# A mixture-of-experts layer on one core: TensorE leaves out the upper half of the second layer where an expert's last tile holds at most 128 rows

## The chip, the cores and the metric

One core of a Trainium2 chip. The metric is the device time of one execution in microseconds. Times inside an execution are counted from the start of its span. TensorE is called PE here, VectorE DVE, ScalarE ACT, GpSimd POOL and SyncE SP; PEld is the weight load of TensorE.

## The reference

The input is (4, 1024, 256) in float32. It is normalised, goes through a small attention block (whose result is added to it), is normalised again, and then goes through eight experts, of which each row uses the two with the largest gate values:

```python
logits = flat @ gate_w + gate_b
topv, topi = lax.top_k(logits, TOP_K)                # TOP_K = 2 of E = 8
topw = softmax(topv)
routing = zeros_like(logits).at[arange(T)[:, None], topi].set(topw)
def body(acc, params):
    W1e, b1e, W2e, b2e, we = params                  # W1e 256 x 1024, W2e 1024 x 256
    h = gelu(flat @ W1e + b1e)
    out = h @ W2e + b2e
    return acc + out * we[:, None], None
final, _ = lax.scan(body, init, (w1, b1, w2, b2, routing.T))
x = x + _layernorm(final)
```

With the inputs of this case the experts 0 to 7 are chosen by 585, 110, 3998, 173, 2449, 188, 554 and 135 rows, 8192 in all.

## The kernel before

The first part (up to about 200 us) computes attention and gate and sends each row, by an indirect DMA, to a place in `sorted_x` that belongs to its expert. `steer_table` then works out on DVE, for each expert, how many tiles of TM = 256 rows it has and which number its first tile has. The result, tiles + 32 * base, is the word that each engine reads from `steer`.

The second part is the loop over experts and tiles. `over_tiles` writes it for each engine: it loads the word of expert e, calls `first` for the first tile and `tile` for the others. Experts are taken from the busiest on, so that slot e0 is expert 2, e1 is expert 3, and so on to e7, which is expert 1. Two tiles of e0 are done ahead of the loop. What is left are 14, 1, 10, 1, 3, 1, 3 and 1 tiles for the slots e0 to e7, 34 in all. The slots e0 to e5 share one piece of program (a loop over three pairs, with a copy for each of the two slots of a pair); e6 and e7 have a copy each. On PE (`roomy=True`) a slot has three copies of the tile's body: one in `first`, one in a loop over groups of four tiles, and one in a loop over the tiles that are left ("singles"), in which each turn asks whether there is such a tile and jumps over the body if not.

All products are made of three float32r products: the operands are split in a high part and a low rest. For a tile PE does this:

- layer 1: 48 matmuls `pL<-xeT,w` (L1420), in four banks of 12
- four transposes `pX<-ident,xt` of the next tile's rows (L417)
- layer 2: 48 matmuls `pY<-w,h` (L1432). Both 128-row halves of the tile are done, and the two are interleaved: for each chunk c of 128 hidden units three matmuls for the lower half (i = 0) and three for the upper (i = 1). Ahead of each second chunk PE waits for `h_split`.

ACT applies gelu to a bank as soon as PE has it (L1360). DVE splits each bank into `h_hi` (L1449) and `h_lo` (L1451) and signals `h_split` after each of the four. Then it makes `xeT_lo` of the next tile (L422), takes the tags, and, for each half i after `l2_done`, adds the bias, takes off the mean and weighs the rows (`take_rows`, L1470 to L1478). POOL adds the rows to `sum_y` with an indirect DMA, one for each half (L492). In the first tile of a slot, ACT and DVE also split the next slot's weights (L171, L178): DVE has two such pieces ahead of the banks, one after bank 1, one after bank 3, one before each half of `take_rows` and two at the end.

When all tiles are done, SP waits for the last rows, loads the sums, and the last norm and the stores follow.

## Time and profile before

| | us |
|---|---|
| runs | 665.25, 668.15, 670.36 |
| median of the runs | 668.15 |
| the profiled execution | 667.14 |
| its span | 665.4 |
| PE busy | 554.9 (83%) |
| DVE busy | 485.5 (73%) |
| ACT busy | 290.4 (44%) |
| POOL busy | 183.7 (28%) |

The span is the time from the first to the last recorded instruction; 1.7 us of the profiled execution lie outside it. The duration of a matmul in the records (0.28 us) is longer than the distance from one matmul to the next (0.11 us), because matmuls are pipelined: distances between starts are what counts. The idle time before an instruction stands in brackets, with what ended it. Where that is an engine that had been done for long, or "issue", the engine's own sequencer was at work: branches and register instructions are recorded under the names of the queues (PEldq, DVEq, POOLq).

### The profile page before, as it was taken

What the parts mean: (1) busy time and instruction counts of PE and PEld (TensorE: products, weight loads), DVE (VectorE), ACT (ScalarE), POOL (GpSimd) and SP (SyncE); (2) the same over time, 40 slices, a digit from 0 to 9 for tenths busy, and PEclk for the clock granted to TensorE, in tenths of its full rate; (3) what the DMA queues carried; (4) which work ended last, traced back from release to release, by engine and by line L of the source; (5) the groups of instructions that cost most, each with busy time, mean ns of one, the idle gap of its engine ahead of it and who ended that gap; (6) DMA issues with size and microseconds to landing.
All of it is one profiled execution on the core that took longest, in us unless ns stands there. A gap on an engine that the chain in (4) does not pass through costs nothing.

```text
span 665.4 us, 14536 instructions
## 1 busy us (share of the span) xinstructions
PE 554.9 (83%) x4170; PEld 503.6 (76%) x4175; DVE 485.5 (73%) x1579; ACT 290.4 (44%) x669; POOL 183.7 (28%) x153
## 2 busy tenths in 40 slices
PE   2868868688587989999999989999999999999600
PEld 1637354363567979999999979999999999899500
DVE  5858889688958777766767677667675796796457
ACT  3354756667453532333333345333333643652250
POOL 2000062350714652323223231132222322232300
PEclk9967968888788999999999999999999999999855
DMA  7920021380305833322323265223232562532386
GB/s 207 364 94 0 1 88 40 101 295 1 112 34 177 232 89 48 54 41 49 47 48 48 49 171 156 40 50 46 48 48 48 161 170 48 158 47 52 45 288 223
DMA packets 51853, 66.81 MB, mean 100 GB/s; under 512 B 4870, under 2 KB 45292, under 8 KB 51692
## 3 DMA queue, kind: packets, MB, share of 16 engines
q1 hardware_dynamic: 37804, 47.87, 23.0%
q0 software_dynamic: 14016, 18.56, 16.3%
q8 instruction: 14, 0.23, 0.1%
q14 instruction: 19, 0.16, 0.1%
HBM read 38.26 MB, written 28.74 MB: 101 GB/s over the span
## 4 chain that ended last, share of the span: by engine, by line
PE 61%; DVE 16%; issue 7%; ACT 6%; DMA 5%; DVEq 1%; POOL 1%; ACTq 0%; SPq 0%; POOLq 0%
PE pY L1432 26%; PE pL L1420 22%; PE pP L697 4%; DMA sum_y<-y,dest 2%; PE pP L798 2%; PE pS L714 2%; ACT xn L544 2%; PE pX L417 2%; DVE z L1580 2%; PE pT L682 1%; DMA w_stage<-sum_y 1%; ACT xrow L611 1%; DVE w_lo L178 1%; POOL sum_y L492 1%; DVE x_all L1001 1%
## 5 line engine op out<-in xcount | busy, mean ns | idle before, releaser
L1360 ACT ACTIVATE h<-pL,b_now 128x256 f32<-128x256 f32 x272 | 114.1, 471 | 225.1 <-PE pL L1420 224.3
L492 POOL DMA_INDIRECT sum_y<-y,dest x70 | 113.1, 1616 | 284.7 <-DVE y L1478 262.8
L1432 PE MATMUL pY<-w_hi,h_lo 128*128 128x256 f32 x544 | 154.2, 283 | 4.5 <-DVE h_lo L1451 4.4
L1420 PE MATMUL pL<-xeT_hi,w_lo 128*128 128x256 f32 x544 | 152.4, 280 | 6.2 <-issue 6.1
L1420 PE MATMUL pL<-xeT_lo,w_hi 128*128 128x256 f32 x544 | 151.6, 279 | 0.0
L1420 PE MATMUL pL<-xeT_hi,w_hi 128*128 128x256 f32 x544 | 151.5, 279 | 0.0
L1432 PE MATMUL pY<-w_hi,h_hi 128*128 128x256 f32 x544 | 151.1, 278 | 0.0
L1432 PE MATMUL pY<-w_lo,h_hi 128*128 128x256 f32 x544 | 151.1, 278 | 0.0
L1420 PEld LDWEIGHTS pL<-xeT_hi,w_lo 128*128 128x128 f32 x544 | 103.0, 189 | 7.5 <-issue 7.1
L1432 PEld LDWEIGHTS pY<-w_hi,h_lo 128*128 128x128 f32 x544 | 102.5, 188 | 6.2 <-DVE h_lo L1451 6.1
L1420 PEld LDWEIGHTS pL<-xeT_hi,w_hi 128*128 128x128 f32 x544 | 103.1, 189 | 0.0
L1420 PEld LDWEIGHTS pL<-xeT_lo,w_hi 128*128 128x128 f32 x544 | 103.0, 189 | 0.0
L1432 PEld LDWEIGHTS pY<-w_lo,h_hi 128*128 128x128 f32 x544 | 102.6, 189 | 0.0
L1432 PEld LDWEIGHTS pY<-w_hi,h_hi 128*128 128x128 f32 x544 | 102.5, 188 | 0.0
L1451 DVE TENSOR_TENSOR h_lo<-h,h_hi 128x512 fp32r<-128x512 f32 x136 | 94.3, 693 | 4.7
L163 POOL DMA_INDIRECT sorted_x<-xrow,slot_i x48 | 46.9, 976 | 134.3 <-DVE xrow L1062 120.6
L1449 DVE CAST h_hi<-h 128x512 fp32r<-128x512 f32 x136 | 61.0, 448 | 28.7 <-ACT h L1360 28.0
L1470 DVE SCALAR_TENSOR_TENSOR y<-pY,b_all 128x256 f32<-128x256 f32 x68 | 28.6, 420 | 51.3 <-PE pY L1432 51.3
L178 DVE TENSOR_TENSOR w_lo<-w_stage,w_hi 128x512 fp32r<-128x512 f32 x64 | 42.2, 684 | 13.6 <-issue 13.1
L171 ACT ACTIVATE w_hi<-w_stage 128x512 fp32r<-128x512 f32 x64 | 37.2, 630 | 3.9 <-DMA w_stage<-w 3.9
L682 PE MATMUL pT<-ident,xn 128*128 128x128 f32 x64 | 16.7, 432 | 18.7 <-ACT xn L544 11.1
L563 ACT ACTIVATE qk<-pP 128x512 bf16<-128x512 f32 x32 | 19.1, 597 | 26.8 <-PE pP L697 26.8
(249 smaller groups left out, 839.0 us busy)
## 6 DMA issues: line engine op xcount, KB each, us to landing
w_stage<-w SPq DMA_DIRECT2D x16, 1024.0 KB, 9.0
xt<-sorted_x SPq DMA_DIRECT2D x38, 260.0 KB, 2.7
sum_y<-fill SPq DMA_DIRECT2D x1, 4352.0 KB, 19.7
w_stage<-sum_y SPq DMA_DIRECT2D x8, 512.0 KB, 7.7
out<-z SPq DMA_DIRECT2D x8, 512.0 KB, 3.0
x_all<-x SPq DMA_DIRECT2D x3, 1024.0 KB, 8.6
sorted_x<-fill SPq DMA_DIRECT2D x8, 260.0 KB
sum_y<-y,dest POOLq DMA_INDIRECT x70, 3.8
```

Of the source, the lines that this page charges most:

```text
L163: pool.indirect_dma_start(out=sorted_x, out_offset=bass.IndirectOffsetOnAxis(ap=slot_i[:, i:i + 1], axis=0), in_=rows[:, i % TB, :], in_of ...
L171: act.activation(w_hi[par][:, i, q * WQ:(q + 1) * WQ], w_stage[par][:, i, q * WQ:(q + 1) * WQ], ACT.Copy).then_inc(w_hi_ready[i], 1)
L178: low = dve.tensor_tensor(w_lo[par][:, i, piece], w_stage[par][:, i, piece], w_hi[par][:, i, piece].bitcast(F32), ALU.subtract)
L492: pool.indirect_dma_start(out=sum_y, out_offset=bass.IndirectOffsetOnAxis(ap=to[:, i:i + 1], axis=0), in_=rows[:, i, :], in_offset=None, c ...
L682: mm = pe.transpose(pT[:, n % 2, u * P:(u + 1) * P], xn[:, t, k * P:(k + 1) * P], ident[:])
L697: mm = pe.matmul(pP[:, n % 2, :], w[:, k, i, mo], x[:, k, tok], start=(k == 0 and w is wqk_lo), stop=(k == KC - 1 and x is xT_lo))
L1360: a = act.activation(h[:, c, :], pL[:, bk, i * TM:(i + 1) * TM], ACT.Gelu, bias=b1_now[par][:, c:c + 1])
L1420: mm = pe.matmul(pL[:, bk, i * TM:(i + 1) * TM], w[:, 0, col], x[:, k, :], start=(k == 0 and w is lo), stop=(k == KC - 1 and x is xeT_lo))
L1432: mm = pe.matmul(pY[:, i, 0:D], s[:, c, rows], w[:, 1, c * D:(c + 1) * D], start=(c == 0 and s is h_lo), stop=(c == FC - 1 and w is lo))
L1449: dve.tensor_copy(h_hi[:, cs, :], h[:, cs, :]).then_inc(h_hi_ready, 1)
L1451: dve.tensor_tensor(h_lo[:, cs, :], h[:, cs, :], h_hi[:, cs, :].bitcast(F32), ALU.subtract).then_inc(h_split, 1)
L1470: dve.scalar_tensor_tensor(out=y[:, i, :], in0=pY[:, i, 0:D], scalar=1.0, in1=b2_all[:, bass.ds(who, 1), :].rearrange("p e d -> p (e d)"), ...
```

## The change

`steer_table` also works out whether the last tile of an expert has more than 128 rows. It counts half tiles (`halves`), takes `full = halves - 2 * tiles`, which is 1 if so and 0 if not, and puts it into bit 11 of the word; every engine now masks the word's fields. PE's layer 2 is written in another order: first all eight chunks of the lower half, with the four waits for `h_split`, then all eight of the upper half. In `first` and in the singles, the upper half stands under a condition. If the tile is the last and `full` is 0, one matmul stands in its place; its result is not used by any row that counts, and it signals `l2_done` as the half would have done. So that the last tile is always one of the singles, that loop has four turns instead of three (`left` is 1 to 4), and the groups of four take the rest. The three slots whose last tile has at most 128 rows are e4 (554 - 512 = 42 rows), e6 (585 - 512 = 73) and e7 (110).

```diff
@@ steer_table
-                count, tiles, incl, base, keep = (cnt[:, i, 0:NE] for i in range(5))
+                count, tiles, incl, base, keep, halves, full, word = (cnt[:, i, 0:NE] for i in range(8))
...
                 ch(dve.tensor_scalar(cnt_i[:, 0, :], count, float(TM - 1), None, ALU.add))
+                dve.tensor_scalar(cnt_i[:, 2, :], cnt_i[:, 0, :], int(np.log2(P)), None, ALU.arith_shift_right)
                 ch(dve.tensor_scalar(cnt_i[:, 1, :], cnt_i[:, 0, :], int(np.log2(TM)), None,
                                      ALU.arith_shift_right))
+                dve.tensor_copy(halves, cnt_i[:, 2, :])
                 ch(dve.tensor_copy(tiles, cnt_i[:, 1, :]))
+                dve.scalar_tensor_tensor(out=full, in0=tiles, scalar=-2.0, in1=halves, op0=ALU.mult, op1=ALU.add)
                 ch(dve.tensor_tensor_scan(incl, keep, tiles, float(AHEAD), ALU.mult, ALU.add))
+                dve.scalar_tensor_tensor(out=word, in0=full, scalar=float(1 << FULL_AT), in1=tiles,
+                                         op0=ALU.mult, op1=ALU.add)
                 ch(dve.tensor_tensor(base, incl, tiles, ALU.subtract))
@@ over_tiles, expert
-                n, base = both & 31, both >> 5
+                n, base, odd = both & 31, (both >> 5) & 63, (both >> FULL_AT) & 1
...
-                    first(e, who, pair, par, base)
+                    if roomy:
+                        first(e, who, pair, par, base, (n * 2 + odd, 2))
+                    else:
+                        first(e, who, pair, par, base)
                     with eng.If(n >= 2):
                         if roomy:
-                            fours = (n + 31) & 28
-                            with eng.If(n >= 5):
+                            fours = (n + 30) & 28
+                            with eng.If(n >= 6):
...
-                            with eng.Fori(0, 3) as v:
-                                with eng.If(((n + 3) & 3) > v):
-                                    tile(e, who, par, singles + v)
+                            left = ((n + 2) & 3) + 1
+                            with eng.Fori(0, 4) as v:
+                                with eng.If(left > v):
+                                    tile(e, who, par, singles + v, (left * 2 + odd, v * 2 + 2))
@@ tensor, tile
-                for c in range(FC):
-                    if c % 2 == 0:
-                        pe.wait_ge(h_split, 4 * g + c // 2 + 1 + ONE)
-                    for i in range(TM // P):
-                        rows = slice(i * P, (i + 1) * P)
-                        for s, w in ((h_lo, hi), (h_hi, hi), (h_hi, lo)):
-                            mm = pe.matmul(pY[:, i, 0:D], s[:, c, rows], w[:, 1, c * D:(c + 1) * D],
-                                           start=(c == 0 and s is h_lo), stop=(c == FC - 1 and w is lo))
-                        if c == FC - 1:
-                            mm.then_inc(l2_done, 1)
+                for c in range(0, FC, 2):
+                    pe.wait_ge(h_split, 4 * g + c // 2 + 1 + ONE)
+                    mm = second_rows(par, 0, range(c, c + 2))
+                mm.then_inc(l2_done, 1)
+                if full is None:
+                    second_rows(par, 1).then_inc(l2_done, 1)
+                    return
+                have, need = full
+                with pe.If(have > need):
+                    second_rows(par, 1).then_inc(l2_done, 1)
+                with pe.If(have <= need):
+                    pe.matmul(pY[:, 1, 0:D], h_hi[:, 0, P:2 * P], hi[:, 1, 0:D],
+                              start=True, stop=True).then_inc(l2_done, 1)
```

`second_rows(par, i, chunks)` is the same three matmuls per chunk for one half i.

In PE's program, in the body of the singles of a pair's first slot, the start of layer 2 was this (the ISA row at L1428 and the register row set the values of the waits for `h_split`; between two of them stand twelve matmuls, six for each half):

```order
687 L1428 ISA
688 L1432 MATMUL pY<-w_hi,h_lo 128x256
...
699 L1432 MATMUL pY<-w_lo,h_hi 128x256
700 L1428 REGISTER_ALU
701 L1432 MATMUL pY<-w_hi,h_lo 128x256
```

Now six matmuls stand between two waits, all of the lower half, and then the upper half follows without a wait, between two branches, and the single matmul between two more:

```order
694 L1447 ISA
695 L1427 MATMUL pY<-w_hi,h_lo 128x256
...
701 L1447 REGISTER_ALU
702 L1427 MATMUL pY<-w_hi,h_lo 128x256
...
721 L1427 MATMUL pY<-w_lo,h_hi 128x256
723 L1454 COMPARE_AND_BRANCH
...
748 L1454 UNCONDITIONAL_BRANCH
749 L1456 COMPARE_AND_BRANCH
750 L1457 MATMUL pY<-w_hi,h_hi 128x256
751 L1456 UNCONDITIONAL_BRANCH
```

The last wait for `h_split` moved from the 36th matmul of layer 2 to the 18th, and four branch instructions came in at the end of the tile.

On DVE, in `steer_table`, the chain from the row counts to the word was this:

```order
L1094 TENSOR_TENSOR cnt<-ends,row 128x8
L1095 TENSOR_SCALAR cnt_i<-cnt 128x8
L1096 TENSOR_SCALAR cnt_i<-cnt_i 128x8
L1098 CAST cnt<-cnt_i 128x8
L1099 SCALAR_TENSOR_TENSOR cnt<-cnt 128x8
L1100 TENSOR_TENSOR cnt<-cnt 128x8
L1102 SCALAR_TENSOR_TENSOR steer<-cnt 1x8
```

Now it is this:

```order
L1096 TENSOR_TENSOR cnt<-ends,row 128x8
L1097 TENSOR_SCALAR cnt_i<-cnt 128x8
L1098 TENSOR_SCALAR cnt_i<-cnt_i 128x8
L1099 TENSOR_SCALAR cnt_i<-cnt_i 128x8
L1101 CAST cnt<-cnt_i 128x8
L1102 CAST cnt<-cnt_i 128x8
L1103 SCALAR_TENSOR_TENSOR cnt<-cnt 128x8
L1104 SCALAR_TENSOR_TENSOR cnt<-cnt 128x8
L1105 SCALAR_TENSOR_TENSOR cnt<-cnt 128x8
L1107 TENSOR_TENSOR cnt<-cnt 128x8
L1109 SCALAR_TENSOR_TENSOR steer<-cnt 1x8
```

Four instructions were put between the others, none with a wait of its own; nothing else moved there.

## Rows read from the trace of the kernel before

**Rows 1.** The page: TensorE's granted clock by slices, the chain that ended last.

```profile
PEclk9967968888788999999999999999999999999855
...
PE 61%; DVE 16%; issue 7%; ACT 6%; DMA 5%; DVEq 1%; POOL 1%; ACTq 0%; SPq 0%; POOLq 0%
```

**Rows 2.** Timeline of PE, a tile of e2: layer 2, then the next tile's layer 1.

```profile
439.23 0.37 PE L1432 MATMUL pY<-w_hi,h_lo 128*128 128x256 f32 x1
...
444.77 0.28 PE L1420 MATMUL pL<-xeT_hi,w_lo 128*128 128x256 f32 x1
444.88 0.28 PE L1420 MATMUL pL<-xeT_hi,w_hi 128*128 128x256 f32 x1
```

**Rows 3.** Timeline of DVE in that tile: what follows the fourth split at once.

```profile
441.01 0.68 DVE L422 TENSOR_TENSOR xeT_lo<-pX,xeT_hi 128x512 fp32r<-128x512 f32 x1
```

**Rows 4.** Timeline of PE: layer 2 begins late (tile 2 of e0, first of e5, first of e6).

```profile
237.85 0.38 PE L1432 MATMUL pY<-w_hi,h_lo 128*128 128x256 f32 x1 [0.90 <-DVE h_lo L1451]
249.40 0.66 PE L417 MATMUL pX<-ident,xt 128*128 128x128 f32 x4 [0.38 <-DMA xt<-sorted_x]
...
572.02 0.39 PE L1432 MATMUL pY<-w_hi,h_lo 128*128 128x256 f32 x1 [1.63 <-DVE h_lo L1451]
584.57 0.38 PE L1432 MATMUL pY<-w_hi,h_lo 128*128 128x256 f32 x1 [0.65 <-DVE h_lo L1451]
```

**Rows 5.** Timeline of DVE: the same in tile 2 of e0 and in e5.

```profile
241.03 0.68 DVE L422 TENSOR_TENSOR xeT_lo<-pX,xeT_hi 128x512 fp32r<-128x512 f32 x1
575.67 0.68 DVE L178 TENSOR_TENSOR w_lo<-w_stage,w_hi 128x512 fp32r<-128x512 f32 x1
```

**Rows 6.** Timeline of PE: the first matmul of e1, of e2 and of e5.

```profile
381.49 0.38 PE L1420 MATMUL pL<-xeT_hi,w_lo 128*128 128x256 f32 x1 [1.24 <-issue]
396.91 0.57 PE L1420 MATMUL pL<-xeT_hi,w_lo 128*128 128x256 f32 x1 [3.23 <-issue]
563.94 0.38 PE L1420 MATMUL pL<-xeT_hi,w_lo 128*128 128x256 f32 x1 [0.23 <-issue]
```

**Rows 7.** PE's sequencer by line: ns minimum/median/maximum, first and last start in us.

```profile
L1263 PEldq ALU_OP  x12: 32/34/36, 378.1 to 611.8; - x12
L1264 PEldq ALU_OP  x2: 36/36/36, 378.6 to 379.4; - x2
L1254 PEldq COMPARE_BRANCH  x7: 67/217/3705, 391.4 to 623.7; - x7
...
L1254 PEldq COMPARE_BRANCH  x1: 3546/3546/3546, 391.4 to 391.4; - x1
```

**Rows 8.** Stretch after e1: busy PE, PEld, DVE, ACT, POOL; clock, DMA share, GB/s.

```profile
397.00:400.00 3.00, 3.00 (x14) 3.00 (x15) 1.93 (x4) 0.08 (x1) 1.76 (x2) 0.50 0.72 83
```

**Rows 9.** Timeline of DVE: end of e6's last tile, all of e7.

```profile
612.79 0.42 DVE L1470 SCALAR_TENSOR_TENSOR y<-pY,b_all 128x256 f32<-128x256 f32 x1 [2.11 <-PE pY L1432]
...
614.42 0.41 DVE L1478 TENSOR_SCALAR y<-y,y_mean,weight 128x256 f32<-128x256 f32 x1
618.80 0.43 DVE L1449 CAST h_hi<-h 128x512 fp32r<-128x512 f32 x1 [3.97 <-ACT h L1360]
...
624.40 0.17 DVE L426 COPY tag<-xt 128x8 f32<-128x8 f32 x1
625.83 0.42 DVE L1470 SCALAR_TENSOR_TENSOR y<-pY,b_all 128x256 f32<-128x256 f32 x1 [1.26 <-PE pY L1432]
```

**Rows 10.** The chain that ended last, its part behind e7.

```profile
614.50 0.07 DVEq L1270
...
629.61 3.75 DMA sum_y<-y,dest
```

**Rows 11.** Timeline of DVE in `steer_table`, and of PE behind it.

```profile
204.89 0.15 DVE L1102 SCALAR_TENSOR_TENSOR steer<-cnt 1x8 int32<-1x8 f32 x1
204.98 0.21 DVE L1107 TENSOR_SCALAR gm<-cnt,place 128x8 f32<-128x8 f32 x1
...
209.24 0.55 PE L763 MATMUL pS<-w_hi,h_lo 128*128 128x256 f32 x1 [1.47 <-DVE h_lo L954]
```

34 lines of the change are left out of this document (22 added, 12 removed).

## The prediction

> **What bounds the kernel now.** I read the page first. The chain that ended last is PE for 61% of the span, and the granted clock is at its full level in nearly all slices of the expert loop [rows 1]. So the loop, from about 217 us on, runs at PE's pace where nothing else interferes. The timeline of a tile in the middle of a slot shows that pace: one matmul each 0.11 us (5.54 for 49), and 5.54 us from the start of layer 2 to the next tile's layer 1, with no gap for other engines [rows 2]. The next question is what ends the few gaps there are. There are two kinds. In the first tile of a slot DVE has the next weights to split as well, and PE waits for `h_lo` before layer 2: 1.63 us in e5, 0.65 in e6 [rows 4]. Between slots PE waits for its own sequencer, "issue" [rows 6], and the sequencer's branches show why [rows 7]. A matmul removed thus counts in the middle of a slot, and less where DVE ends last.
>
> **What is removed.** Three tiles (e4's third, e6's third, e7's only one) lose 24 matmuls and get one: 23 x 0.113 = 2.6 us each, 7.8 us in all. This is the most that PE can save.
>
> **The new order in the full tiles.** The last wait for a split stood behind 36 matmuls of the layer, with 12 left; it stands now behind 18, with 30 left (6 of the lower half, 24 of the upper). If the fourth split is ready S after layer 2 began, the layer ended at max(5.5, S + 1.4) before and ends at max(5.5, S + 3.4) now; the new order costs nothing while S is under about 2.1. In a tile in mid-slot the fourth split ends at 441.01, 1.8 after the start at 439.23 [rows 2, 3]: no cost, with 0.3 to spare, in some 20 tiles. Where DVE is late, it costs: in tile 2 of e0, S is 241.03 - 237.85 = 3.2 and in e5's 575.67 - 572.02 = 3.65 [rows 4, 5], so that by this rule PE ends 1.2 and up to 1.6 us later (3.4 + 3.2 or 3.65, less 5.5, with 0.1 for the semaphore). Such tiles are the first three of e0 and the first ones of e1, e3, e4, e5 and e6. Of e0's, 0.9 remains when DVE has caught up, since tile 2 began with a wait for DVE anyway and tile 3's transposes no longer wait 0.38 for their transfer. In return DVE can take the lower half's rows while PE does the upper half: `take_rows` is 1.0 per half (both from 612.79 to 614.83) [rows 9], so DVE is done 1 us sooner after a full tile's end. A PE that is late therefore pays little in the next first tile.
>
> **The way out of a slot.** The singles loop turns four times instead of three. A turn without a tile costs the sequencer 379.4 - 378.6 = 0.8 us [rows 7]. It came out of e0's last body at 378.1, 1.9 us ahead of the last matmul's start (381.49 - 1.24 - 0.28 = 379.97), because matmuls are queued ahead; with two empty turns and the loading of the next word this lead was used up and PE stood 1.24; after e4, with one empty turn, 0.23 [rows 6]. So one more empty turn adds 0.8 at the ends of e0, e2, e4 and e6. The conditions add four branches per tile in `first` and singles. A branch not taken is about 0.07 and one taken 0.21 (least and median) [rows 7]: 0.45 per tile, hidden by the lead where the next tile follows, not hidden at a slot's end. I take 1.25 at the end of e0, e2, e4 and e6, and 0.45 behind e1 and e3. The bounds are 0 (all in the lead's cover) and 1.6 (the two branches around the upper half taking 0.2 more each).
>
> **Steering.** Four DVE instructions without a wait, 0.09 each (204.89 to 204.98), lie on the path, since PE stands 1.47 us for the split behind them [rows 11]: 0.4 us. The masks on the other engines are two register instructions per slot; DVE, POOL and SP have them once per slot in stretches of some microseconds of branches; I take them at nothing, at most 0.1 per slot.
>
> **The sum along the loop,** as lateness against before. e0: PE 0.9, after its exit 2.1. e1: DVE's fourth split comes just when PE wants it; 2.1, and 0.45 behind it: 2.6. e2: 2.6, after its exit 3.8. In e3 and in e4's first two tiles PE had waited for DVE some tenths here and there, which now falls into the lateness, and the order adds some: layer 2 of e4's third tile begins 3.1 late. That layer was 5.5 long and is 2.8 now (24 matmuls and one), a gain of 2.7: PE and DVE leave it 0.4 late, PE with the exit 1.6. In e5 PE had waited 1.63 for DVE [rows 4]; now both arrive nearly together, 0.4 late, and the layer ends 3.4 after the fourth split: 575.67 + 0.1 + 0.4 + 3.4 = 579.6. By the rule of before it would have ended at 572.02 + 5.5 = 577.5, with the waits inside the layer some tenths later, so this is 1.7 late. e6's first tile ends 3.4 after its fourth split too, about 2.0 late, while DVE is still 0.4 late; the third tile's layer 2 begins 1.9 late. The half tile takes off 2.6: DVE is through with `take_rows` 0.7 early. From here DVE decides. Its way through its empty turns to e7 begins at once (614.50) and lasts until 618.80, though the row names ACT, which had long been done [rows 9, 10]; its four splits and the tag follow until 624.5, and there it stood 1.26 for PE [rows 9]. PE has 23 matmuls less to do there and is ready first. So e7's rows go out 0.7 + 1.3 = 2.0 early. The scatter (3.75 us) [rows 10], the loading of the sums and the last norm follow unchanged. With 0.4 for the steering, 1.6 us are left of the 7.8. The profiled execution of 667.14 would be 665.5; the median of the runs is 1.0 above it, so I forecast **666.5**. The bounds of this sum: with exits at nothing the same chain gives 3.5 less (664.6), with exits at 1.6 about 1 less (667.2).
>
> **A rule against this change.** In e1 the branch over the whole part for more tiles took 3.5 us, and the same one in e7, the last to run, 3.7, where the median is 0.22 [rows 7]; PE stood 3.23 for the first [rows 6]. The Trainium skill, "Runtime: NRT & Kernel Launch", section "Instruction fetch mechanics", says that a taken branch whose target isn't in the fetched pages waits for a DMA that fetches it. That would fit two branches in code that had not been run yet. By that rule new jumps in code seen for the first time could each stall.
>
> **Rivals.**
> *Fetch stalls (slower).* Place: the new taken branches at the end of `first` and singles, the first time each copy is run (e0's two, e1's, e6's two, e7's: six). Price: 3.5 less the lead of 1.9, 1.6 each, 9.8 in all, if nothing behind takes it up; with the rest -1.6 + 9.8 = +8.2, **676.3**. It ends slower than before from two such stalls on, and measurably so with five or six. Against it: the new jumps pass over 1 matmul or 24, the two long ones over the whole part for further tiles, with two more bodies of 100; the empty turns jump over one such body each way within 0.8.
> *The clock.* Behind e1 PE had stood 3.23 us, and from 397 to 400 the granted clock was 0.50, which is 1.2 GHz [rows 6, 8]; 14 matmuls went in those 3 us, 0.21 each instead of 0.11, so 1.4 was lost. After 1.24 us it stayed at 2.4 GHz. The gaps behind e0 and e2 become 2.5. If both pull the clock down, 2.8 is lost, and DVE follows: +1.2, **669.3**.
> *The gain arrives whole.* If the order costs nothing (DVE's slack turns up everywhere) and the exits are covered: -7.8, **660.4**. Against it: S of 3.2 and 3.65 [rows 4, 5].
> *The short way isn't taken* (the flag reads full for all): the costs alone, -1.6 + 7.8 at most, **674.3**.
>
> **How the numbers follow.** Forecast 0.60, the clock 0.19, gain whole 0.08, fetch stalls 0.11, short way not taken 0.02. The range runs from between the gain's whole and my sum (661.5) to two thirds of the fetch stalls (673.5). 1%, 6.7 us, is about what a measurement of this kernel can tell from no change: the runs before lie between 665.25 and 670.36. Faster than that (under 661.5) needs nearly the whole gain: 0.06. Slower (over 674.8) needs nearly all the fetch stalls: 0.09. Within 1%: 0.85.
>
> **What the changed profile would show.** The layer 2 matmuls in the loop fall from 34 x 48 = 1632 to 1563. In mid-slot tiles layer 2 still lasts 5.54 us; if it is more, the slack of 0.3 was too small, and with 20 tiles this would be the worst error. Layer 2 of e5's and e6's first tiles ends 3.4 after the fourth split. The gaps behind e0 and e2 are about 2.5, those behind e4 and e6 about 1.5, and a new branch of over 3 us anywhere speaks for the fetch. e7's `take_rows` no longer waits for PE. Clock at 0.50 anywhere but behind e1 speaks for the second rival.

## The result and the profile after

The changed kernel takes **682.82 us** (median of 4 runs, 680.82 to 683.30) against 666.96 us for the kernel before in the same comparison (665.25 to 670.36). The ratio is **1.0228, 95% interval 1.0194 to 1.0262**: 15.2 us slower by the ratio, 15.9 between the medians. A run more than 1.5% above the fastest of the same kernel is left out of a ratio; this concerns only four of the ten runs of e6_dyn below. The forecast was 666.5 with a range up to 673.5, so it was wrong, and on the side of a rival to which it gave 0.11. The profiled execution took 680.82 us, its span is 678.7.

The page of the changed kernel, against [rows 1]:

```profile
PEclk9978978688797999999999889999998899999855
...
q8 instruction: 18, 0.29, 0.2%
...
PE 68%; DVE 14%; issue 7%; ACT 6%; DMA 3%; DVEq 0%; POOL 0%; ACTq 0%; SPq 0%; POOLq 0%
```

The clock row has four 8s in the loop, in two places, where before had 9s. The queue q8, which carries instructions, moved 14 packets before and moves 18 now, of 16 KB each. Both turn out to matter.

The matmuls first. The groups of layer 1 and 2 say where the time went. The columns are busy time and mean ns, then the idle time ahead of the group and what ended it. Before:

```profile
L1432 PE MATMUL pY<-w_hi,h_lo 128*128 128x256 f32 x544 | 154.2, 283 | 4.5 <-DVE h_lo L1451 4.4
L1420 PE MATMUL pL<-xeT_hi,w_lo 128*128 128x256 f32 x544 | 152.4, 280 | 6.2 <-issue 6.1 <-DVE xeT_lo L422 0.2
```

After:

```profile
L1440 PE MATMUL pL<-xeT_hi,w_lo 128*128 128x256 f32 x544 | 157.4, 289 | 22.7 <-issue 22.4 <-DVE xeT_lo L424 0.2
```

TensorE stood 6.2 us ahead of a layer 1 before and stands 22.7 now, nearly all of it "issue", its own sequencer. The busy time of this third of layer 1 rose by 5.0 with the same number of matmuls; the clock rows below show why. The places are the first matmuls of e1 to e7, against [rows 6] (timeline of PE, idle time in brackets):

```profile
383.83 0.38 PE L1440 MATMUL pL<-xeT_hi,w_lo 128*128 128x256 f32 x1 [2.88 <-issue]
400.99 0.38 PE L1440 MATMUL pL<-xeT_hi,w_lo 128*128 128x256 f32 x1 [3.48 <-issue]
521.04 0.45 PE L1440 MATMUL pL<-xeT_hi,w_lo 128*128 128x256 f32 x1 [2.86 <-issue]
538.43 0.58 PE L1440 MATMUL pL<-xeT_hi,w_lo 128*128 128x256 f32 x1 [3.71 <-issue]
574.99 0.39 PE L1440 MATMUL pL<-xeT_hi,w_lo 128*128 128x256 f32 x1 [3.11 <-issue]
592.11 0.38 PE L1440 MATMUL pL<-xeT_hi,w_lo 128*128 128x256 f32 x1 [3.43 <-issue]
628.93 0.38 PE L1440 MATMUL pL<-xeT_hi,w_lo 128*128 128x256 f32 x1 [2.98 <-issue]
```

Every way out of a slot now costs 2.9 to 3.7 us. Before, it was 1.24 behind e0, 3.23 behind e1 and 1.12 behind e2; behind e3 and e5 there was no gap at all, and behind e4 and e6 0.23 and 0.26. The sequencer's rows, against [rows 7] (ns minimum/median/maximum, first and last start; the first row is the branch over an expert's other tiles, the others the singles loop behind e0):

```profile
L1264 PEldq COMPARE_BRANCH  x8: 67/1546/3765, 229.2 to 639.4; - x8
...
L1274 PEldq ALU_OP  x4: 36/36/36, 379.1 to 381.9; - x4
L1274 PEldq COMPARE_BRANCH  x4: 83/214/216, 379.1 to 382.0; - x4
```

The first branch is the one that was L1254 before. Four of eight executions now take 3.0 to 3.8 us (395.5, 532.7, 586.7, 639.4); before, two did (391.4 and 623.7), the first execution of the pair's second slot (e1) and that of e7, which has a copy of its own. The two new ones are the exits of e3 and e5, where the same branch took 0.217 before. The packets of q8 in the trace fit: in each of the four a packet starts 0.6 to 1.5 us after the branch does (396.5, 533.6, 588.2, 640.0). The empty turns behind e0 are three, 0.93 us each (379.1 to 381.9).

The clock, against [rows 8] (columns as there; two stretches behind e0's gap and one in the middle of a slot):

```profile
384.00:386.00 2.00, 2.00 (x13) 2.00 (x14) 0.80 (x2) 0.00 (x0) 0.39 (x1) 0.67 0.82 260
386.00:388.00 2.00, 2.00 (x11) 2.00 (x11) 1.41 (x3) 0.84 (x2) 0.00 (x0) 0.50 0.99 346
...
437.00:439.00 2.00, 2.00 (x20) 2.00 (x20) 0.99 (x4) 0.11 (x1) 1.33 (x1) 1.00 0.52 123
```

Behind the gap the granted clock falls to 0.50 (1.2 GHz) for part of layer 1, and the rows counted are 11 to 13 in 2 us instead of 20. From its first matmul to its last, layer 1 takes 7.1 to 7.2 us there instead of 5.3 to 5.7. This happens behind all seven gaps; before, only behind e1 (7.0).

What went as forecast: a tile in mid-slot, against [rows 2, 3], still takes 5.54 us from layer 2 to the next layer 1, and its fourth split (467.74, 0.69 long) ends 1.9 after the layer began:

```profile
466.56 0.37 PE L1427 MATMUL pY<-w_hi,h_lo 128*128 128x256 f32 x1
...
472.10 0.28 PE L1440 MATMUL pL<-xeT_hi,w_lo 128*128 128x256 f32 x1
```

In the loop's first tile (of e0) VectorE is late, and the lower half waits for a split in its middle, as tile 2 of e0 did at its start before [rows 4]:

```profile
223.65 0.39 PE L1427 MATMUL pY<-w_hi,h_lo 128*128 128x256 f32 x1 [0.18 <-DVE h_lo L1474]
226.38 0.39 PE L1427 MATMUL pY<-w_hi,h_lo 128*128 128x256 f32 x1 [0.71 <-DVE h_lo L1474]
...
230.96 0.28 PE L1440 MATMUL pL<-xeT_hi,w_lo 128*128 128x256 f32 x1
```

The layer lasts 7.31. And the chain at the end, against [rows 10], with 24 of e7's matmuls of layer 2 on it where before it had 45:

```profile
636.85 2.87 PE pY L1427 x24
642.53 1.13 issue
643.66 3.87 DMA sum_y<-y,dest
```

The traces don't settle the 0.4 us taken for the steering from [rows 11]: the loop's first matmul starts at 217.11 instead of 216.97, but two later kernels with the same steering on a chip of this speed (g2_never, g3_twoways) start at 218.24 and 218.59. From there PE stands behind before by 2.3 us at the start of e1, 4.1 at e2's, 6.3 at e3's, 11.1 at e4's, 11.05 at e5's, 14.2 at e6's, 15.6 at e7's, and its last matmul by 13.8. The half tiles give back 2.7 at e4's and 2.6 at e6's third tile and 1.8 in e7 with all that happens there; the exits take more.

The loop is 13.7 us longer from its first matmul to its last. Measured between starts of matmuls in the two traces, this is made up of:

| part | us |
|---|---|
| the seven exits | +16.6 (behind e0 and e2 1.6 and 1.7, behind e3 and e5 3.8 and 3.6, behind e4 and e6 2.9 and 2.7, behind e1 0.3) |
| layer 1 at the slow clock behind them | +9.5 (1.5 to 1.6 each, 1.8 in e6, 0.2 behind e1) |
| layer 2 of the three half tiles | -8.1 |
| waits for VectorE ahead of a first tile's layer 2, which are gone | -4.7 |
| all other tiles, the new order included | +0.4 |

### The profile page after: what moved, and what is told of

It reads as the page before. It is cut to its first block, busy times and chain, and to the rows that moved or that the text cites. A ratio compares the mean times of both kernels' runs of the same rounds, so it can differ in the third digit from the quotient of the medians.

```text
span 678.7 us, 14581 instructions
## 1 busy us (share of the span) xinstructions
PE 557.5 (82%) x4105; PEld 506.5 (75%) x4106; DVE 486.1 (72%) x1583; ACT 290.3 (43%) x669; POOL 181.7 (27%) x153
## 4 chain that ended last, share of the span: by engine, by line
PE 68%; DVE 14%; issue 7%; ACT 6%; DMA 3%; DVEq 0%; POOL 0%; ACTq 0%; SPq 0%; POOLq 0%
PE pL L1440 28%; PE pY L1427 25%; PE pP L699 4%; PE pP L800 2%; PE pX L419 2%; PE pS L716 2%; ACT xn L546 2%; DMA sum_y<-y,dest 2%; DVE z L1603 2%; PE pT L684 1%; ACT xrow L613 1%; PE pS L765 1%; DVE x_all L1003 1%; PE pT L794 1%; DVE mstats L1008 1%
## 5 line engine op out<-in xcount | busy, mean ns | idle before, releaser
L1440 PE MATMUL pL<-xeT_hi,w_lo 128*128 128x256 f32 x544 | 157.4, 289 | 22.7 <-issue 22.4
L1440 PE MATMUL pL<-xeT_lo,w_hi 128*128 128x256 f32 x544 | 156.0, 287 | 0.0
L1440 PE MATMUL pL<-xeT_hi,w_hi 128*128 128x256 f32 x544 | 155.9, 287 | 0.0
L1427 PE MATMUL pY<-w_hi,h_lo 128*128 128x256 f32 x520 | 148.2, 285 | 1.8 <-DVE h_lo L1474 1.5
L1427 PE MATMUL pY<-w_hi,h_hi 128*128 128x256 f32 x520 | 144.6, 278 | 0.0
L1427 PE MATMUL pY<-w_lo,h_hi 128*128 128x256 f32 x520 | 144.5, 278 | 0.0
L1440 PEld LDWEIGHTS pL<-xeT_hi,w_hi 128*128 128x128 f32 x544 | 107.7, 198 | 0.0
L1427 PEld LDWEIGHTS pY<-w_hi,h_lo 128*128 128x128 f32 x520 | 97.9, 188 | 3.2 <-DVE h_lo L1474 3.2
L1427 PEld LDWEIGHTS pY<-w_lo,h_hi 128*128 128x128 f32 x520 | 98.1, 189 | 0.0
L1501 DVE TENSOR_SCALAR y<-y,y_mean,weight 128x256 f32<-128x256 f32 x68 | 29.3, 431 | 2.5
```

The costliest lines, as they stand in the source:

```text
L1427: mm = pe.matmul(pY[:, i, 0:D], s[:, c, rows], w[:, 1, c * D:(c + 1) * D], start=(c == 0 and s is h_lo), stop=(c == FC - 1 and w is lo))
L1440: mm = pe.matmul(pL[:, bk, i * TM:(i + 1) * TM], w[:, 0, col], x[:, k, :], start=(k == 0 and w is lo), stop=(k == KC - 1 and x is xeT_lo))
L1501: dve.tensor_scalar(y[:, i, :], y[:, i, :], y_mean[:, i:i + 1], weight[:, i:i + 1], ALU.subtract, ALU.mult).then_inc(y_ready, 1)
```

## The experiments

Sixteen kernels ran, four at a time, each four beside runs of the kernel before on the same chip. Three of the four chips run the kernel before in about 700 us instead of 667; nearly all of the difference lies ahead of the expert loop, which begins at 247 to 254 us there instead of 217. So two measures are given: the ratio to the kernel before on the same chip, and the length of the loop in the one profiled execution, from the first matmul of layer 1 of e0 to the last of layer 2 of e7 (before: 216.97 to 625.75, 408.8). "Long" counts the executions over 2.9 us of the branch over an expert's other tiles; packets are q8's.

| kernel | ratio (95%) | us, from ratio | loop | long | packets |
|---|---|---|---|---|---|
| before | 1 | 0 | 408.8 | 2 | 14 |
| changed | 1.0228 (1.0194 to 1.0262) | +15.2 | 422.5 | 4 | 18 |
| e1_order | 1.0066 (1.0034 to 1.0098) | +4.7 | 419.4 | 2 | 14 |
| e2_turns | 1.0056 (1.0031 to 1.0081) | +3.9 | 415.1 | 2 | 14 |
| e3_never | 1.0250 (1.0200 to 1.0301) | +17.6 | 432.0 | 4 | 18 |
| e4_pad | 0.9997 (0.9971 to 1.0022) | -0.2 | 408.9 | 2 | 14 |
| e5_three | 1.0153 (1.0087 to 1.0220) | +10.7 | 421.1 | 4 | 18 |
| e6_dyn | 1.0015 (0.9969 to 1.0062) | +1.0 | 417.7 | 4 | 18 |
| e7_pad1 | 1.0017 (0.9984 to 1.0050) | +1.2 | 411.2 | 2 | 14 |
| e8_dynb | 1.0019 (0.9995 to 1.0044) | +1.3 | 411.6 | 2 | 14 |
| f1_jump2 | 1.0150 (1.0129 to 1.0171) | +10.5 | 420.5 | 4 | 18 |
| f2_jump1 | 1.0010 (0.9991 to 1.0030) | +0.7 | 409.4 | 2 | 14 |
| f3_firstfull | 1.0039 (1.0006 to 1.0073) | +2.7 | 413.7 | 2 | 14 |
| f4_oldorder | 0.9932 (0.9907 to 0.9956) | -4.8 | 402.4 | 2 | 14 |
| g1_after | 1.0229 (1.0181 to 1.0276) | +15.3 | 424.2 | 4 | 18 |
| g2_never | 1.0023 (0.9999 to 1.0047) | +1.5 | 410.2 | 2 | 14 |
| g3_twoways | 0.9940 (0.9911 to 0.9968) | -4.0 | 401.8 | 2 | 15 |
| g4_early | 1.0020 (0.9997 to 1.0043) | +1.3 | 409.6 | 2 | 14 |

The third column is the ratio less one, times the median of before on that chip. The loop of one execution scatters by some microseconds (e1_order's profiled run was the slowest of its seven). In the lists of gaps of e1_order, e2_turns and e5_three, in f1_jump2 and in the count at the end, a gap is the distance from one matmul to the next less the usual 0.11; this is about 0.2 more than the idle time in brackets, which is meant elsewhere.

One place makes the chips differ inside the loop too. From the loop's first matmul to the third layer 2 of e0 it takes 31.7 to 33.1 us on the two sets of runs at 667, in the changed kernel (32.59 and 33.05) as in the kernel before (32.84); on the slower chips it takes 33.6 to 35.6 in kernels with the old order and 36.3 to 39.0 in those with the new one.

### First four: the change taken apart

**e1_order**, the new order of layer 2 alone:

```diff
-                for c in range(FC):
-                    if c % 2 == 0:
-                        pe.wait_ge(h_split, 4 * g + c // 2 + 1 + ONE)
-                    for i in range(TM // P):
-                        rows = slice(i * P, (i + 1) * P)
+                for i in range(TM // P):
+                    rows = slice(i * P, (i + 1) * P)
+                    for c in range(FC):
+                        if i == 0 and c % 2 == 0:
+                            pe.wait_ge(h_split, 4 * g + c // 2 + 1 + ONE)
```

> The kernel before with the new order of the second layer alone, in every tile: the lower half's 24 matmuls with the waits between them, then the upper half's 24 without a wait. No condition, no change of the loop. Theory (the exits, the code that is fetched and the clock behind the gaps made the change slow, not the order): the waits for the split cost 0.7 us at most, once, at the end of the first expert; the gaps behind the experts stay at about 1.2, 3.2, 1.1, 0, 0.2, 0, 0.3 us; 666 to 669 us. Rival (the order starves TensorE between banks and VectorE's evictions of the lower half come too late): a good part of the 15 us is here already, 672 us or more.

Measured: +4.7 us (2.4 to 6.9). Neither account held as written: the exits do stay (1.36, 3.58, 1.27, 0.01, 0.47, 0.02, 0.20), but the order isn't nearly free. It costs in tiles where VectorE is late. e3's tile (timeline of PE, a wait inside the lower half; then VectorE behind its last split):

```profile
568.73 0.39 PE L1432 MATMUL pY<-w_hi,h_lo 128*128 128x256 f32 x1 [0.69 <-DVE h_lo L1450]
```

```profile
569.04 0.69 DVE L1450 TENSOR_TENSOR h_lo<-h,h_hi 128x512 fp32r<-128x512 f32 x1
569.65 0.68 DVE L178 TENSOR_TENSOR w_lo<-w_stage,w_hi 128x512 fp32r<-128x512 f32 x1
```

That layer takes 7.30 instead of 5.85, and e0's second tile 12.3, where the kernels with the old order show 7.0 to 8.5 on these chips. e0's third layer 2 begins at 39.02 after the loop's first matmul, in e4_pad on the same chip at 35.43: 3.6 us of the order's cost lie there, and these don't show in the result (32.59 against 32.84).

**e2_turns**, the loop with four turns alone:

```diff
-                            fours = (n + 31) & 28
-                            with eng.If(n >= 5):
+                            fours = (n + 30) & 28
+                            with eng.If(n >= 6):
...
-                            with eng.Fori(0, 3) as v:
-                                with eng.If(((n + 3) & 3) > v):
+                            left = ((n + 2) & 3) + 1
+                            with eng.Fori(0, 4) as v:
+                                with eng.If(left > v):
```

> The kernel before with the new loop over the tiles alone: four turns for the single tiles instead of three, and one to four of them run. No condition on the half, the old order of the second layer. Theory (each empty turn takes about 0.8 us of TensorE's sequencer, so every expert's exit is 0.8 later, and it shows where the queued matmuls don't cover it): the gaps behind the first and the third expert (one tile less in the fours) grow by 0.8 to 2.5 and to 4.0, behind the fifth and the seventh to 0.5 to 1.5 from nearly 0; behind a gap that passes 2.8 us the first 16 matmuls of the next layer 1 run at 0.21 us each and cost 1.6 more; +2 to +6 us, 669 to 673. Rival (the whole of the 15 us hangs on the conditions of the half): 667 to 668. If the long branches of 3.4 to 3.8 us behind the fourth and the sixth expert are here too, the loop's form brings them and not the half.

Measured: +3.9 us, as the theory had it. The gaps behind e0, e2, e4 and e6 are 2.53, 2.48, 1.43 and 1.49 from one matmul to the next, each 1.0 to 1.2 more than in e4_pad (1.41, 1.32, 0.39, 0.28). The first matmuls of e1 and e3, and a stretch behind e3's and one behind e1's:

```profile
422.22 0.38 PE L1421 MATMUL pL<-xeT_hi,w_lo 128*128 128x256 f32 x1 [2.36 <-issue]
...
556.87 0.38 PE L1421 MATMUL pL<-xeT_hi,w_lo 128*128 128x256 f32 x1 [2.31 <-issue]
```

```profile
557.00:559.00 2.00, 2.00 (x13) 2.00 (x14) 0.00 (x0) 0.00 (x0) 1.70 (x2) 0.70 0.44 98
423.00:425.00 2.00, 2.00 (x19) 2.00 (x18) 0.34 (x1) 0.84 (x2) 1.58 (x2) 1.00 0.81 324
```

Of two gaps of the same length one brought the slow clock and one did not. No new long branch.

**e3_never**, the changed program with the short way never taken:

```diff
-                dve.scalar_tensor_tensor(out=full, in0=tiles, scalar=-2.0, in1=halves, op0=ALU.mult, op1=ALU.add)
+                dve.scalar_tensor_tensor(out=full, in0=tiles, scalar=0.0, in1=keep, op0=ALU.mult, op1=ALU.add)
```

> The changed kernel with one number different: the bit that tells whether the last tile is full is always 1, so the short way is never taken, while every condition, empty turn and instruction of the changed program stays. It leaves nothing out of the result. Theory: the three half tiles take their 24 matmuls again (3 times 2.6 = 7.8 us of work), but at the exits of the fifth and the seventh expert these matmuls cover part of the sequencer's way, so the gaps there shrink from 3.7 and 3.4 to about 1.9 and lose the slow clock behind them (1.6 each): the balance is +0 to +3 us against the changed kernel, 683 to 686. The long branches behind the second, fourth, sixth and last expert stay. Rival (the exits cover nothing and the whole 7.8 us had been gained, only lost elsewhere): 690 us or more.

Measured: 1.0250 against 1.0228 and 1.0229 for the changed kernel. The 69 matmuls left out (7.8 us of TensorE) are thus worth about 1.4 us in the changed kernel, which its intervals can't tell from nothing. Part of where they go is seen at the exits of e4 and e6 (first matmuls of e5 and e7):

```profile
619.63 0.39 PE L1440 MATMUL pL<-xeT_hi,w_lo 128*128 128x256 f32 x1 [1.85 <-issue]
...
674.35 0.38 PE L1440 MATMUL pL<-xeT_hi,w_lo 128*128 128x256 f32 x1 [1.59 <-issue]
```

With the matmuls there, these gaps are 1.85 and 1.59 with layer 1 at full clock behind them; without, 3.11 and 2.98 with layer 1 at 7.2 us: 1.3 of gap and 1.5 of clock, against 2.6 saved. The sequencer's place shows why. Where it comes out of e4's last tile, with that tile's last matmul, first here, then in the changed kernel:

```profile
L1274 PEldq ALU_OP  x1: 36/36/36, 615.9 to 615.9; - x1
617.51 0.28 PE L1427 MATMUL pY<-w_lo,h_hi 128*128 128x256 f32 x1
```

```profile
L1274 PEldq ALU_OP  x1: 36/36/36, 571.2 to 571.2; - x1
571.59 0.28 PE L1457 MATMUL pY<-w_hi,h_hi 128*128 128x256 f32 x1
```

Behind a full tile it stands 1.6 us ahead of the last matmul, behind a half tile 0.4 (0.3 behind e6's).

**e4_pad**, longer code that is never run:

```diff
+                            if par == 1 and type(e) is not int:
+                                with eng.If(n >= 31):
+                                    for _ in range(17):
+                                        eng.matmul(pY[:, 0, 0:D], h_hi[:, 0, 0:P], w_hi[par][:, 1, 0:D],
+                                                   start=True, stop=True)
```

> The kernel before, with 17 more matmuls in the code of the loop's second slot, under a condition that is never true (an expert with 31 tiles or more), so that the pair's loop is longer by about as many instructions as in the changed kernel (36) and executes the same work in the same order. It leaves nothing out. Theory (the length or the place of the loop's code decides whether the far jump over an expert's other tiles finds its target in TensorE's instruction buffer): the jumps behind the fourth and the sixth expert take over 3 us each as in the changed kernel, where they took 0.2 in the kernel before; the gaps there grow from 1.1 and 0.2 to about 3 and bring the slow clock behind them; +5 to +10 us, 672 to 678. Rival (the length doesn't matter; the stalls come from the new jumps themselves, or from what was jumped over shortly before): 667 to 668, both jumps at 0.2.

Measured: no change, and the branch behind e3 is as short as before (its row):

```profile
L1254 PEldq COMPARE_BRANCH  x1: 217/217/217, 562.6 to 562.6; - x1
```

My theory, that the 36 further instructions bring the long branches, fell. (The gaps in the kernel before that the expectation gives as 1.1 and 0.2 are those behind e2 and e4; behind e3 and e5 there was none.)

### Next four: the exits

**e5_three**, the changed kernel with before's number of turns:

```diff
-                            fours = (n + 30) & 28
-                            with eng.If(n >= 6):
+                            fours = (n + 31) & 28
+                            with eng.If(n >= 5):
...
-                            left = ((n + 2) & 3) + 1
-                            with eng.Fori(0, 4) as v:
+                            left = (n + 3) & 3
+                            with eng.Fori(0, 3) as v:
```

> The changed kernel (short last tiles and their conditions) on the loop of the kernel before: three turns for the single tiles, two empty ones behind the first and the third expert and one behind the fifth and the seventh, where the changed kernel has three and two. With this input no expert's last tile falls into the fours, so all three half tiles still take the short way. Theory (an empty turn is worth 0.93 us of the changed kernel's exits): gaps of about 2.1 behind the first and the third expert, 2.4 and 2.2 behind the fifth and the seventh, the slow clock behind some of them gone: 4 to 9 us below the changed kernel. On the long branches (3.4 to 3.8 us behind the fourth and the sixth expert): the loop is 34 instructions longer than in the kernel before and its jump stands 28 later. If the conditions or the place of the jump bring them, they are here too: 5 to 11 us above the kernel before. Rival (four turns and conditions together bring them): 0.2 each, and -2 to +3 us against the kernel before.

Measured: +10.7 us (6.1 to 15.4, four runs), 4.5 less than the changed kernel's +15.2. The gaps are 1.79, 1.77, 2.28 and 2.07 behind e0, e2, e4, e6. The long branches are there (3.41 and 3.23 us), so the conditions bring them, or the place of the jump.

**e6_dyn**, a loop over the single tiles with its end in a register. (The expectation says "on every engine"; only TensorE has this form of the loop, and only its program changed.)

```diff
                             left = ((n + 2) & 3) + 1
-                            with eng.Fori(0, 4) as v:
-                                with eng.If(left > v):
-                                    tile(e, who, par, singles + v, (left * 2 + odd, v * 2 + 2))
+                            with eng.Fori(0, left) as v:
+                                tile(e, who, par, singles + v, (left * 2 + odd, v * 2 + 2))
```

> The changed kernel with a loop over the single tiles that runs just as often as there are tiles (its end in a register), on every engine: no empty turn and no condition around each turn. Theory (the exits were dear because of the empty turns): gaps behind the first and third expert from 3.0 to below 0.6, behind the fifth and the seventh from 3.3 and 3.1 to about 1.4, each without the slow clock behind it (1.6 each): 12 to 16 us below the changed kernel, -2 to +4 us against the kernel before; the long branches behind the second, fourth and sixth expert stay (3.6 to 3.9 with the slow clock behind them). Rival (the condition on the half, with its reads of registers, is what drains TensorE, not the turns): gaps stay above 2 and the gain against the changed kernel is below 6 us.

Measured: +1.0 us by the ratio, 14 less than the changed kernel, but this figure is the weakest of the table. The ten runs spread from 697.2 to 714.1 (before on that chip: 694.8 to 704.5), and the ratio goes by the six under 708; the median of all ten, 706.48, is 6.9 above before's, and the profiled run took 705.74. What its trace shows is firmer. The first matmuls of e1 and e5:

```profile
414.02 0.38 PE L1439 MATMUL pL<-xeT_hi,w_lo 128*128 128x256 f32 x1
...
600.89 0.38 PE L1439 MATMUL pL<-xeT_hi,w_lo 128*128 128x256 f32 x1 [1.36 <-issue]
```

The gap behind e0 is gone, those behind e4 and e6 are 1.4, all with full clock. The long branches behind e3 and e5 stay, with the slow clock behind them.

**e7_pad1**, the padding in the first slot, so that the far jump stands where it stands in the changed kernel:

```diff
+                            if par == 0 and type(e) is not int:
+                                with eng.If(n >= 31):
+                                    for _ in range(14):
+                                        eng.matmul(pY[:, 0, 0:D], h_hi[:, 0, 0:P], w_hi[par][:, 1, 0:D],
+                                                   start=True, stop=True)
```

> The kernel before with 14 more matmuls in the code of the loop's first slot, under a condition that is never true, so that the second slot's far jump stands at the place where it stands in the changed kernel (29 instructions later) and the loop's end near its place too. It leaves nothing out. Theory (the place of the jump decides whether its target is still in the instruction buffer: by then the next stretch of code has been fetched or not): branches of over 3 us behind the fourth and the sixth expert, +5 to +10 us. Rival (the place doesn't matter; the small taken jumps within the tiles, which this kernel doesn't have, bring the long branches): 0.2 us each, -1 to +1 us.

Measured: no change that can be told, and 0.215 us for the branch behind e5. The place of the jump doesn't matter either.

**e8_dynb**, the same loop in the kernel before (in TensorE's program alone, here too):

```diff
-                            with eng.Fori(0, 3) as v:
-                                with eng.If(((n + 3) & 3) > v):
-                                    tile(e, who, par, singles + v)
+                            left = (n + 3) & 3
+                            with eng.If(left >= 1):
+                                with eng.Fori(0, left) as v:
+                                    tile(e, who, par, singles + v)
```

> The kernel before with the loop over the single tiles running just as often as there are tiles, under a condition for none, on every engine; no half tiles. Theory (an empty turn costs the sequencer 0.9 us and shows where the queued matmuls don't cover it): the gaps behind the first and the third expert shrink from 1.4 and 1.3 to about 0, those behind the fifth and the seventh from 0.4: 2 to 4 us below the kernel before. Rival (the sequencer's lead was lost on something else, or VectorE's work behind the exit sets the start of the next expert's layer 2): -1 to +1 us.

Measured: +0.2%, no gain; the rival was right. The two groups of TensorE, in e7_pad1 (which runs as the kernel before does, on the same chip), then here:

```profile
L1437 PE MATMUL pY<-w_hi,h_lo 128*128 128x256 f32 x544 | 155.0, 285 | 4.0 <-DVE h_lo L1456 4.0
L1425 PE MATMUL pL<-xeT_hi,w_lo 128*128 128x256 f32 x544 | 152.6, 280 | 7.0 <-issue 6.7 <-DVE xeT_lo L422 0.2
```

```profile
L1433 PE MATMUL pY<-w_hi,h_lo 128*128 128x256 f32 x544 | 155.6, 286 | 8.0 <-DVE h_lo L1452 8.0
L1421 PE MATMUL pL<-xeT_hi,w_lo 128*128 128x256 f32 x544 | 152.4, 280 | 3.2 <-issue 3.2
```

The exits give back 3.8 us and the wait for `h_lo` in the next tile takes 4.0. In the kernel before, the gaps behind e0, e2, e4 and e6 lay in the shadow of VectorE, which sets the first tile of the next slot. Only what goes beyond that shadow costs.

### Third four: what makes the far branch long

**f1_jump2** and **f2_jump1**: the kernel before with one small jump more, behind the first tile of the second slot (`par == 1`) or of the first (`par == 0`):

```diff
                     first(e, who, pair, par, base)
+                    if roomy and par == 1 and type(e) is not int:
+                        with eng.If(n >= 31):
+                            eng.matmul(pY[:, 1, 0:D], h_hi[:, 0, P:2 * P], w_hi[par][:, 1, 0:D],
+                                       start=True, stop=True)
                     with eng.If(n >= 2):
```

> The kernel before with one small jump more: in the loop's second slot, between the first tile and the far jump over the other tiles, a condition that is never true around one matmul, so that a short taken jump stands right ahead of the far jump, as in the changed kernel. It leaves nothing out. The length of the code and the place of the far jump have been ruled out by then. Theory (a taken jump within the tile, just ahead of the far one, makes the sequencer give up the code behind the far jump): branches of over 3 us behind the fourth and the sixth expert, 18 instruction packets instead of 14, gaps of about 3.4 there, +4 to +8 us. Rival (it takes the jumps of all tiles together, or what is jumped over): 0.2 us each, 14 packets, -1 to +1 us.

> The same small jump in the loop's first slot instead, behind its first tile, far ahead in time of the far jump of the second slot. It leaves nothing out. Theory (only a taken jump right ahead of the far one counts): 0.2 us at the far jumps behind the fourth and sixth expert, 14 packets, -1 to +1 us. Rival (any further taken jump in the loop's code pushes a stretch of it out): over 3 us each, 18 packets, +4 to +8 us. If neither this kernel nor its twin shows them, the jumps alone don't bring them.

Measured: **+10.5 us (9.1 to 12.0) for the one, +0.7 (-0.6 to 2.1) for its twin**. Both theories that named the second slot were right, though the first had the size at 4 to 8. In f1_jump2 the small branch itself is cheap (first row, with e1, e3 and e5), and the far one behind e3 and behind e5 is long (the next two):

```profile
L1255 PEldq COMPARE_BRANCH  x3: 224/224/224, 427.9 to 617.3; - x3
...
L1258 PEldq COMPARE_BRANCH  x1: 3175/3175/3175, 562.5 to 562.5; - x1
...
L1258 PEldq COMPARE_BRANCH  x1: 3315/3315/3315, 617.6 to 617.6; - x1
```

e4's first matmul, and the clock behind it:

```profile
567.53 0.57 PE L1424 MATMUL pL<-xeT_hi,w_lo 128*128 128x256 f32 x1 [3.20 <-issue]
```

```profile
568.00:570.00 2.00, 2.00 (x11) 2.00 (x11) 1.52 (x3) 0.00 (x0) 1.56 (x1) 0.50 0.71 82
570.00:572.00 2.00, 2.00 (x12) 2.00 (x11) 0.75 (x3) 0.84 (x2) 0.00 (x0) 0.50 0.89 227
```

So 10.5 us hang on two branches: 3.36 and 3.12 of gap, and 2.7 and 2.9 since layer 1 lasts 8.3 and 8.2. That is 12.0, less the waits for VectorE of 0.9 each that follow there in f2_jump1 and are gone here. In f2_jump1 the branch behind e5, and e4's first matmul:

```profile
L1258 PEldq COMPARE_BRANCH  x1: 217/217/217, 610.2 to 610.2; - x1
```

```profile
562.36 0.38 PE L1424 MATMUL pL<-xeT_hi,w_lo 128*128 128x256 f32 x1
```

The instruction queue tells the same: 18 packets of 16 KB in the one, 14 in the other, and over all eighteen kernels 18 exactly where four branches are long and 14 or 15 where two are. A long branch thus goes with a fetch. The times of the packets in the trace add two things. In each further long branch one packet starts about 1 us after the branch (563.4 and 618.5 here). The other one comes much earlier, while the slot's first tile runs (552.9 and 606.6 here, 525.1 and 576.7 in the changed kernel), 8 to 11 us ahead of the branch and ahead of the small jump of that turn. So part of the code had been lost before that small jump ran; it can't be what drove this part out.

**f3_firstfull**, e6_dyn without the condition in first tiles, the last expert's excepted, so that no small jump stands ahead of the far ones:

```diff
-                        first(e, who, pair, par, base, (n * 2 + odd, 2))
+                        first(e, who, pair, par, base, (n * 2 + odd, 2) if is_last(e) else None)
```

> The changed kernel with the loop over the single tiles that runs as often as there are tiles, and without the condition on the half in an expert's first tile, except for the last expert. All three half tiles of this input still take the short way (they are the last single tiles of the fifth and the seventh expert, and the only tile of the last). No small jump is left ahead of the far jumps. Theory: branches behind the fourth and the sixth expert back to 0.2 us, their gaps from 3.4 to below 0.3 and the slow clock behind them gone; most of the 10 us at these two places comes back, less what VectorE's lateness in the next tile hides: 4 to 9 us below the kernel with that loop and all conditions, 2 to 8 us below the kernel before. Rival (the long branches stay, since the jumps in the single tiles bring them too): within 2 us of the kernel before.

**f4_oldorder**, the same with before's order in every tile without a condition:

```diff
+                if full is None:
+                    for c in range(FC):
+                        if c % 2 == 0:
+                            pe.wait_ge(h_split, 4 * g + c // 2 + 1 + ONE)
+                        for i in range(TM // P):
+                            mm = second_rows(par, i, (c,))
+                            if c == FC - 1:
+                                mm.then_inc(l2_done, 1)
+                    return
```

> The same kernel, but the tiles without a condition (an expert's first tile except the last expert's, and the fours) have the layer 2 of the kernel before, both halves chunk by chunk; only the single tiles and the last expert's first have the lower half ahead of the upper. Theory (the new order costs about 4.7 us by itself, in tiles where VectorE is late with the splits, and these are mostly first tiles and the tiles of the first expert): 2 to 5 us below its twin, 5 to 11 us below the kernel before. Rival (the cost of the order was of the first kernel's chance placement, or sits in the single tiles): no difference from the twin, -1 to +1 us.

Measured: +2.7 us for the first, so my number of 2 to 8 us faster was wrong, and -4.8 (-6.5 to -3.1) for the second, just short of the 5 to 11 that I expected. The branches behind e3 and e5 take 0.22 in both, and their gaps are 0.3 at most. But f3_firstfull was to be 4 to 9 us below e6_dyn, and by the ratios it isn't below it at all (+2.7 against +1.0, on two chips). By the loops (413.7 and 417.7) and by the medians of all runs (+3.0 and +6.9) it is 4 below, the low end. One reason is in the traces: with the exit gone, the order's cost comes out behind it (layer 2 of e4's and e6's first tiles 6.74 and 6.67 instead of 5.44 and 5.62). So the long branches' 10.5 us and the order's cost don't add up where they meet.

What I had too low is the order. Between these twins it is 7.5 us by the ratios and 11.3 by the loops, and their traces place the 11.3: 3.8 from the start of e0 to the third layer 2 (37.95 against 34.16) and 0.8 more to the last, 1.6 in e1 (layer 2 of 7.38 against 5.74) and 0.5 at its exit, 0.7 from e2 to the third tile of e4 and 1.2 from there to the third of e6. Another 2.7 lies in the clock behind e1 (layer 1 of e2 8.33 against 5.64), which changes from run to run. Most of the tiles that lose are those where VectorE has weights to split besides. f4_oldorder's first matmuls of e4 and e5:

```profile
561.01 0.38 PE L1439 MATMUL pL<-xeT_hi,w_lo 128*128 128x256 f32 x1
...
596.54 0.38 PE L1439 MATMUL pL<-xeT_hi,w_lo 128*128 128x256 f32 x1 [1.43 <-issue]
```

### Last four: the sum, and what the matmuls are worth

**g1_after** is the changed kernel again, unedited.

> The changed kernel itself, once more, beside the experiments' kernels. If the costs found so far add up (order +4.7, four turns +3.9, the long branches behind the fourth and the sixth expert +10.7 as with the one small jump, less about 2 for the matmuls left out and plus the cover that is lost with them), it stands 14 to 18 us above the kernel before here too, a ratio of 1.020 to 1.026. Rival (a cost is missing or counted twice): outside of that.

Measured: 1.0229 (1.0181 to 1.0276), the same as the first time, and within what was expected. The parts measured alone: order 4.7, turns 3.9, long branches 10.5 are 19.1, each with 1.5 to 2.3 of uncertainty; e3_never, which has them all and every matmul, shows 17.6 (14.1 to 21.2). That fits, but it doesn't prove that they add up: f3_firstfull shows that they overlap, and by the traces the order makes e0's last layer 2 begin 4.0 and 4.6 us later on the slower chips (e1_order against e4_pad, f3_firstfull against f4_oldorder), but 0.6 and 1.8 at the speed of the result (the changed kernel against before, g1_after against g4_early).

**g2_never**: f4_oldorder with the bit always 1 (the edit of e3_never).

> The fastest version so far (loop that runs as often as there are single tiles; no condition in first tiles but the last expert's; the order of before in tiles without a condition), with the bit for a full last tile always 1: every instruction stays, the short way is never taken, nothing is left out of the result. It tells what the 3 x 23 matmuls left out are worth. Theory (about 2.6 us each, less what is lost: at the exits of the fifth and seventh expert a gap of 1.6 us opens that these matmuls would cover, and VectorE's lateness in the next tile hides part; at the very end all 2.6 count): 3 to 6 us slower than its twin, ratio to the kernel before 0.998 to 1.002. Rival (the gain came from the loop and not from the matmuls): within 1.5 us of the twin, about 0.994.

Measured: 1.0023 (0.9999 to 1.0047), against 0.9932 for the twin and 0.9940 for g3_twoways, which ran beside it. So the matmuls left out are worth 0.83 to 0.91%, **5.5 to 6 us of the 7.8**, once the exits are out of the way (the intervals allow 3 to 8).

**g3_twoways**: two whole layers in a tile with a condition, both halves in before's order or the lower alone:

```diff
+                have, need = full
+                with pe.If(have > need):
+                    both_halves()
+                with pe.If(have <= need):
+                    for c in range(0, FC, 2):
+                        pe.wait_ge(h_split, 4 * g + c // 2 + 1 + ONE)
+                        mm = second_rows(par, 0, range(c, c + 2))
+                    mm.then_inc(l2_done, 1)
+                    pe.matmul(pY[:, 1, 0:D], h_hi[:, 0, P:2 * P], hi[:, 1, 0:D],
+                              start=True, stop=True).then_inc(l2_done, 1)
```

> The fastest version so far, with two whole layers 2 in each tile that has a condition: both halves chunk by chunk as in the kernel before if the tile is full, the lower half alone if not. So the new order stands nowhere in a full tile; TensorE's code is 260 instructions longer. Theory (the order costs 0.6 and 1.2 us in the middle tiles of the fifth and the seventh expert, 6.18 and 6.71 us instead of 5.6): 1 to 2 us below its twin, ratio 0.990 to 0.992. Rival (the longer code brings more fetches at the exits, or the condition ahead of the layer drains TensorE): 2 us or more above its twin.

Measured: 0.9940 (0.9911 to 0.9968), faster than before but not told from f4_oldorder, where 1 to 2 us less were expected. The layers of the middle tiles fell to 5.57 and 5.56 as thought, and the exit behind e4 to 0.65; VectorE takes it back in the next tile.

**g4_early**: the small jump ahead of the first tile of the second slot instead of behind it.

> The kernel before with the small jump in the second slot ahead of its first tile instead of behind it. It leaves nothing out. Theory (the last taken jump ahead of the far one counts, wherever it stands): this is now the last jump, so long branches behind the fourth and the sixth expert and +8 to +12 us, as with the jump behind the tile. Rival (it has to stand close to the far jump, in time or in the code): 0.2 us at both, -1 to +1 us.

Measured: no change that can be told, the far branches at 0.22, 14 packets. The small jump (three times 0.207) is now the last taken one ahead of the far one, with about 100 matmuls between, and does nothing. My theory of the last jump fell. Of the places tried, only the one between the second slot's first tile and the far branch has the effect.

## Why the prediction was wrong

**The matmuls removed: right.** 1563 of layer 2 are left, and a half tile's layer takes 2.93 to 3.06 instead of 5.5.

**The order in mid-slot: right** (5.54, nothing). **The rule for late tiles: right** in form: with the fourth split at 3.7 the layer lasts 7.31 (3.4 + 3.7 is 7.1). **The 0.9 for e0 was about right** on the chip of the result (counted from the loop's first matmul, e0's last layer 2 begins 0.6 us later, in g1_after 1.8), and too small for the slower ones, where the order costs 4.7 alone and 7.5 between the twins f3_firstfull and f4_oldorder. In the changed kernel the other places hide it: the first tiles of e5 and e6, whose late splits [rows 4, 5] the sum charged, have no wait there any more, since TensorE comes later than VectorE. For the same reason VectorE doesn't decide at e7, as the sum had it [rows 9]; its rows go out 14 us late (the DMA at 643.66 instead of 629.61), not 2.0 early.

**An empty turn: nearly right.** I took 0.8; it is 0.93. With the conditions I took 1.25 for the exits of e0 and e2; they grew by 1.6 and 1.7. That the turns alone cost 3.9 where 4 x 0.8 was forecast is partly luck: the four gaps grew by 1.0 to 1.2 each, one of them brought 1.5 of slow clock, and VectorE hid part.

**The exit behind a half tile: this step failed.** The prediction took the sequencer's lead of 1.9 us as given. But the lead is the queue of matmuls issued and not yet run, and a half tile takes 23 of them out of that queue just ahead of an exit: the lead there is 0.4 and 0.3, where it is 1.6 behind full tiles (1.9 before, without the conditions). I wrote 1.5 for the gaps behind e4 and e6; they are 3.11 and 2.98, while e3_never with the matmuls has 1.85 and 1.59. Half of what the change saves in the tile it lays open behind it.

**"0.45 behind e1 and e3", and nothing behind e5: this step failed most.** I weighed fetch stalls, but at the new small jumps, and only the first time each is run. The new small jumps take 0.07 to 0.35 us. What stalls is the old far branch, each time behind e3 and e5 (3.58 and 3.77 us instead of 0.217). f1_jump2 shows that one small taken jump between the tile and this branch is enough, and that it costs 10.5 us by itself, against 15.2 for the whole change; in the changed kernel's own trace the gaps of 3.7 and 3.4 behind e3 and e5 and the clock behind them are 10.7 of the 26.1 that exits and clock add. The row was there: the same branch took 0.217 in e3 and e5 and 3.5 in e1 [rows 7]. (The one in e7, which the prediction calls the same, is e7's own copy.) It should have asked what keeps the target at hand in the one case, and priced its loss at 3.5 and the clock, not at 1.6.

By the Trainium skill, "Runtime: NRT & Kernel Launch", section "Instruction fetch mechanics", a taken branch whose target isn't in the fetched pages waits for a fetch. The trace agrees: two more 16 KB packets for each further long branch. The same section says that only two pages of 16 KiB are held and that prefetch is sequential, though it also gives TensorE 128 KiB. By two pages the same branch at the same place would be long each time or never; before, it took 3.5 us in e1 and 0.217 in e3 and e5 [rows 7], over two bodies of about 100 matmuls each, and q8 carried no packet between 396.2 and 585.7, while e2 to e5 ran.

**The clock: the rival was right in kind and too small.** It was put at two gaps of 2.5, 1.4 each. It came behind seven gaps of about 3, six of them new, with 1.5 to 1.8 each. It is the reason why exits of 2 and of 3 us differ by so much more than 1.

**The shadow of VectorE, which the sum had and didn't use.** e8_dynb shows that before's exits of 0.3 to 1.4 cost nothing that can be told. The costs begin where an exit passes the time that VectorE needs for the next weights and splits. In the changed kernel 4.7 us of the exits disappear in this way.

**What stays open.** Why a small jump close ahead of the far one makes its target be fetched again, in the next turns, and the same jump ahead of the tile does not. The length of the code and the place of the far branch were ruled out (e4_pad, e7_pad1), the short way itself too (e3_never). Nor did I find what decides whether a gap between 2.2 and 2.6 us brings the slow clock.

## What to carry to other kernels

Count what a removed piece of work was covering: matmuls ahead of a loop's exit are the sequencer's lead, and taking them away opens the exit (here by 1.3 us for 2.6 us of matmuls, and by 1.5 of slow clock behind it). In a loop with far jumps, look for branches of one line with two very different times: the short ones are short because no fetch is needed, and one small conditional next to the far jump can end that. The idea of the change was sound: with a loop that has no empty turns, no condition ahead of a far jump, and the new order only where the condition needs it, the same removed matmuls give -0.7% (0.9932, 0.9907 to 0.9956) instead of +2.3%.

## What the runs showed of the hardware

- The far branch on TensorE's sequencer takes 0.22 us in some executions and 2.97 to 3.93 us in others, and each further long branch comes with two more instruction packets of 16 KB, one of which starts about 1 us into the branch.
- A condition that is never true around one matmul (0.22 us by itself) made the far branch behind it long each time it was executed; 100 matmuls further ahead (+1.3 us, 14 packets), or in the other slot (+0.7, 14 packets), it did nothing that can be told.
- TensorE's sequencer comes out of a full tile 1.6 to 2.0 us ahead of the tile's last matmul, and 0.3 to 0.4 ahead where the last 23 matmuls are left out.
- Over all eighteen profiles there are 126 ways from one expert to the next. With gaps counted from matmul to matmul less 0.11, layer 1 took over 6 us behind none of the 83 under 2.2 us, behind 2 of the 3 between 2.2 and 2.6, and behind 37 of the 40 of 3.0 and more. In seven of these it lasted 8.2 to 8.4 instead of 5.3 to 5.7; in f1_jump2 the granted clock was 0.50 in both stretches from 568 to 572.
- A turn of a loop whose condition is false costs TensorE's sequencer 0.93 us with two register operations in it; a loop that ends at a register's value has no such turns, and the gap behind e0 was 0.1 us.
